# Layer norm without separate operations for mean and variance, and a third of the MLP's relus on ScalarE

## The reference

```
t = t + attn(ln(t))            # attention without softmax, 6 heads
t = t + ffn(ln(t))
ln(v)  = (v - mean(v)) / sqrt(var(v) + 1e-5)        # over the 96 numbers
ffn(x) = q16(q16(relu(q16(q8(x) @ q8(W1).T) + q8(b1))) quantised to fp8 @ q8(W2).T) + q8(b2))
```

## Time and profile before

| | |
|---|---|
| median of 3 runs | 4113.82 us (4105.76 to 4116.25) |
| profiled execution | 4110.38 us, its span 4108.6 us |
| busy PE, DVE, POOL, ACT | 3482.1, 3421.2, 2847.0, 2397.9 us (85%, 83%, 69%, 58%) |
| the block of 16 phases | from about 3393 us to the end, some 715 us |
| granted TensorE clock, whole span | 0.931 |

### The profile page before, as it was taken

One profiled execution on the slowest core, in us unless ns is written; L12 is line 12 of the kernel. 1 busy time (PEld: TensorE's weight loads), 2 busy tenths in 40 slices (PEclk: granted clock), 3 DMA queues, 4 the chain that ended last, 5 costly groups with the idle time before them and its releaser, 6 DMA issues. The chain is left out here.

```text
span 4108.6 us, 38662 instructions
## 1 busy us (share of the span) xinstructions
PE 3482.1 (85%) x10080; PEld 1402.5 (34%) x10080; DVE 3421.2 (83%) x4323; ACT 2397.9 (58%) x4121; POOL 2847.0 (69%) x2332
## 2 busy tenths in 40 slices
PE   6899999999999999999999999999860887675765
PEld 2333333333333333333333333333320334453553
DVE  3999999999999999999999999999984004778686
ACT  5666776666666677666666677666632221435445
POOL 3988889999999888999999988899870000213123
PEclk8999999999999999999999999999985999786767
DMA  2555555555556555555545555555458877100001
GB/s 85 166 157 169 163 163 159 164 168 156 160 163 176 164 162 157 156 164 157 156 154 166 162 157 163 151 158 163 145 150 207 240 236 187 47 16 12 20 1 31
DMA packets 296513, 588.62 MB, mean 143 GB/s; under 512 B 82743, under 2 KB 151994, under 8 KB 295142
## 3 DMA queue, kind: packets, MB, share of 16 engines
q1 hardware_dynamic: 229222, 516.93, 42.7%
q10 hardware_dynamic: 67072, 69.23, 6.5%
HBM read 532.16 MB, written 58.28 MB: 144 GB/s over the span
## 5 line engine op out<-in xcount | busy, mean ns | idle before, releaser
L796 POOL TENSOR_TENSOR prod<-states,c_rows 128x512 f32<-128x512 f32 x1536 | 1919.9, 1269 | 183.3 <-DVE states L726 149.2
L726 DVE TENSOR_TENSOR_SCAN states<-decay,carry,bpsum 128x512 f32<-128x512 f32 x1344 | 1676.9, 1259 | 0.0
L455 PE MATMUL ypsum<-prod,identity 128*128 128x512 f32 x3072 | 1596.4, 603 | 0.5 <-POOL prod L796 0.3
L561 ACT ACTIVATE decay<-delta,decay_rate 128x512 f32<-128x512 f32 x1344 | 934.8, 711 | 314.0 <-DVE states L726 309.4
L706 DVE TENSOR_TENSOR bpsum<-bpsum,dx 128x512 f32<-128x512 f32 x1344 | 904.6, 673 | 138.6 <-PE bpsum L448 124.4
L455 PEld LDWEIGHTS ypsum<-prod,identity 128*128 128x128 f32 x3072 | 584.2, 194 | 422.7 <-issue 280.8
L448 PE MATMUL bpsum<-b_rows,select 96*128 96x512 bf16 x1344 | 522.8, 389 | 209.4 <-DVE states L726 206.7
L448 PEld LDWEIGHTS bpsum<-b_rows,select 96*128 96x128 bf16 x1344 | 129.5, 96 | 972.6 <-DVE states L726 689.1
L1662 POOL TENSOR_TENSOR y<-y,b 128x384 f16<-128x384 f16 x64 | 68.3, 1067 | 544.8 <-ACT y L1466 544.8
L561 ACT ACTIVATE bpsum<-delta,decay_rate 128x512 f32<-128x512 f32 x192 | 132.6, 691 | 309.5 <-DVE states L726 308.6
L495 PE MATMUL mm<-h_norm,w_xs 96*128 96x512 f32 x512 | 262.8, 599 | 6.0 <-ACT h_norm L627 6.0
(11 more groups left out here) (194 smaller groups left out, 4555.9 us busy)
## 6 DMA issues: line engine op xcount, KB each, us to landing
c_rows<-bc_map SPq DMA_DIRECT2D x512, 512.0 KB, 3.8
c_rows<-bc_map SPq DMA_DIRECT2D x512, 256.0 KB, 4.0
b_wide<-bc_map ACTq DMA_DIRECT2D x128, 256.0 KB, 4.5
image<-normed_map SPq DMA_DIRECT2D x192, 96.1 KB
depthwise_map<-dw_sums ACTq DMA_DIRECT2D x96, 192.0 KB, 4.3
dw_parts<-depthwise_map SPq DMA_DIRECT2D x16, 1152.0 KB, 14.1
b_wide<-bc_map ACTq DMA_DIRECT2D x128, 128.0 KB, 4.2
normed_map<-padded SPq DMA_DIRECT2D x8, 1155.0 KB, 11.7
```

The lines of the kernel that those rows point to most:

```text
L455: pe.matmul(ypsum[:, group % Y_BANKS, :], identity[:, :], prod[:, n % P_RING, :], start=s == 0, stop=s == STATES - 1).then_inc(summed, 1)
L561: act.activation(into, delta[k % 2][:, g, :], ACT.Exp, scale=decay_rate[:, ORDER[k][0], g, s:s + 1]).then_inc(done, 1)
L726: dve.tensor_tensor_scan(states[:, n % H_RING, :], by, add, carry[:, at, u:u + 1], ALU.mult, ALU.add).then_inc(scanned, 1)
L796: pool.tensor_tensor(prod[:, n % P_RING, :], states[:, n % H_RING, :], c_rows[:, n // C_STATES % C_RING, n % C_STATES, :], ALU.mult).then_ ...
```

## The change

It has three parts. First, `center` no longer has the operation that turns the sum into a mean: one operation computes sum x (-1/96) + source. Second, `variance` ends with the sum of squares, and the root on ACT takes 1/96 as its scale and 1e-5 as its bias, read from a new one-column tile `ln_eps`. DVE sets that tile once at the start, and the three engines that waited for four start counts now wait for five. Third, bias and relu of the third piece of each chunk (k = 2) are made by ACT in place, in one operation after it has waited for its own copy, and counted by a new semaphore. DVE now makes relu 0, relu 1, and then the three casts.

```diff
-                    act.activation(stat[:, 2, tiles], stat[:, 1, tiles], ACT.Sqrt).then_inc(ln_root, 1)
+                    act.activation(stat[:, 2, tiles], stat[:, 1, tiles], ACT.Sqrt, scale=1.0 / C, bias=ln_eps[:, :]).then_inc(ln_root, 1)
...
                             act.activation(hid16[:, i % 4, :], mp[:, i % 2, :], ACT.Copy).then_inc(m_taken, 1)
+                        act.wait_ge(m_taken, i + 1)
+                        act.activation(hid16[:, i % 4, :], hid16[:, i % 4, :], ACT.Relu,
+                                       bias=b1[:, phase_of(p)[1], THIRDS - 1:THIRDS]).then_inc(last_relu, 1)
                         if c > 0:
                             add_up(c - 1)
...
                     chain(dve.tensor_reduce(stat[:, 0, tiles], src, AXIS.X, ALU.add))
-                    chain(dve.tensor_scalar(stat[:, 0, tiles], stat[:, 0, tiles], 1.0 / C, None, ALU.mult))
-                    dve.tensor_tensor(dev[:, tiles, :], src, stat[:, 0, tiles].unsqueeze(2).to_broadcast([128, SLICE, C]),
-                                      ALU.subtract).then_inc(ln_centered, 1)
+                    dve.scalar_tensor_tensor(dev[:, tiles, :], stat[:, 0, tiles].unsqueeze(2).to_broadcast([128, SLICE, C]),
+                                             -1.0 / C, src, ALU.mult, ALU.add).then_inc(ln_centered, 1)
...
-                    chain(dve.tensor_reduce(stat[:, 1, tiles], haug[:, v % 2, tiles, 0:C], AXIS.X, ALU.add))
-                    dve.tensor_scalar(stat[:, 1, tiles], stat[:, 1, tiles], 1.0 / C, LN_EPS, ALU.mult, ALU.add).then_inc(ln_var, 1)
+                    dve.tensor_reduce(stat[:, 1, tiles], haug[:, v % 2, tiles, 0:C], AXIS.X, ALU.add).then_inc(ln_var, 1)
...
-                        dve.wait_ge(hid_relu, i + 1)
+                        if k == THIRDS - 1:
+                            dve.wait_ge(last_relu, CHUNKS * n + c + 1)
+                        else:
+                            dve.wait_ge(hid_relu, 2 * (CHUNKS * n + c) + k + 1)
                         dve.tensor_copy(hid8[:, c % 2, k, :], hid16[:, i % 4, :], saturate=False).then_inc(hid8_ready, 1)
...
-                        for k in range(THIRDS):
+                        for k in range(THIRDS - 1):
...
+                        to_fp8(c, THIRDS - 2)
                         to_fp8(c, THIRDS - 1)
...
                 dve.memset(haug[:, :, :, C:C + 1], 1.0)
-                dve.wait_ge(rest_zero, 4)
+                dve.memset(ln_eps[:, :], LN_EPS).then_inc(rest_zero, 1)
+                dve.wait_ge(rest_zero, 5)
```

More of the change, by code:

```diff
@@ L1200, in batch_phase @@
         stat = sb("stat", [128, 3, TILES])
+        ln_eps = sb("ln_eps", [128, 1])
         gram = sb("gram", [128, 4, C + 1])
@@ L1205, in batch_phase @@
                  "t_full", "t_taken", "m_full", "m_taken", "dve_step", "ln_centered", "ln_squared", "ln_var", "ln_root", "ln_ready",
-                 "gram_full", "gram_step", "small_mm", "hid_relu", "hid8_ready", "y_biased", "t_step",
+                 "gram_full", "gram_step", "small_mm", "hid_relu", "last_relu", "hid8_ready", "y_biased", "t_step",
                  "out0_stored", "out1_stored", "rest_zero"]
@@ L1210, in batch_phase @@
          t_full, t_taken, m_full, m_taken, dve_step, ln_centered, ln_squared, ln_var, ln_root, ln_ready,
-         gram_full, gram_step, small_mm, hid_relu, hid8_ready, y_biased, t_step, out0_stored, out1_stored, rest_zero) = handles
+         gram_full, gram_step, small_mm, hid_relu, last_relu, hid8_ready, y_biased, t_step, out0_stored, out1_stored, rest_zero) = handles
         group_loaded = (group0_loaded, group1_loaded, group2_loaded, group3_loaded)
@@ L1395, in _ @@
                 first = 2 * CONV_GROUPS
-                pe.wait_ge(rest_zero, 4)
+                pe.wait_ge(rest_zero, 5)
                 fuse(0)
@@ L1496, in _ @@
                 first = 2 * CONV_GROUPS
-                act.wait_ge(rest_zero, 4)
+                act.wait_ge(rest_zero, 5)
                 for i in range(first):
```

## The result

| kernel | median us | lowest to highest | profiled execution | its span |
|---|---|---|---|---|
| before | 4113.82 | 4105.76 to 4116.25 | 4110.38 | 4108.6 |
| after | 4070.25 | 4065.90 to 4072.11 | 4072.11 | 4070.3 |

The medians are of five executions each. The ratio is 0.9899 with a 95% interval of 0.9888 to 0.9910, so 41.5 us less (4113.82 x 0.0101). Between the two spans the difference is 38.3 us. The medians are 43.6 us apart because the profile of before was taken in an execution 3.4 us under its median and that of after in one 1.9 us over its own.

What follows compares the result with a forecast made beforehand. DVE, partly standing still for POOL, was taken to bound seven of eight MLP phases. Seven times 3.3 us (23.1) plus 2.7 in attention, 0 in the last phase, made 26 us less: 4088 us, range 4078 to 4104.

Steps and rivals of the forecast that it cites:

- ACT's relu out of the way: MLP chunks: ACT's relu mostly fits a 0.58 us gap before y's eviction, adding 0.10 us to a chunk's loop.
- The last MLP phase: Phase without layer norm: ACT takes the lead; between 1 us less and 2 us more, 0 taken.
- Attention: Attention phases: 1.6 us less in phase 0, 0.2 in phase 1, 0.9 in six others; sum 2.7 us.
- The one behind about 0.3: Last chunk of an MLP phase, behind the five loop periods: about 0.3 us less.
- The walk: Chunk-by-chunk path through an MLP phase, pricing the third relu at 0.26 us: 2.5 us less a phase.
- the loop: MLP chunk cycle through casts, TensorE, ACT, POOL's pair and DVE: 5.34 us before, 4.98 after, 5.08 with ACT's part.
- the lower end: Gain per MLP phase from following the chunk cycle: 2.5 us; 3.3 taken, as one relu would pass before POOL's pair.
- the upper end: Gain per MLP phase from work taken off DVE: 2.1 + 0.84 + 0.76 = 3.7 us.
- The lock eats it: Rival, MLP phases: an earlier DVE only waits longer for POOL; 15 us less in all, 4099; chance 0.19.
- DVE slips past POOL: Rival, MLP chunks: two relus and a cast pass before POOL's pair; 33 us less in all, 4081; chance 0.14.
- Two passes: Rival, layer norm: fused centering makes two passes, 0.8 us more each, 26 us, all the gain; 4113; chance 0.06.
- the relu on ACT becomes the loop: Rival, MLP chunks: y, POOL and DVE queue behind ACT's relu; at 1.5 us 16 us slower, 4130; chance 0.04.

Runs made afterwards that it cites:

- e5: Changed kernel with ACT's relu of the third piece made twice, the second on its own result: 4085.69 us, ratio to before 0.9935.
- e6: Changed kernel, but ACT makes the third relu only in each MLP phase's last chunk, DVE in the others: 4085.48 us, ratio to before 0.9938.
- e10: Kernel before with only DVE's order changed to three relus, then three casts; no relu moved, layer norm as it was: 4106.77 us, ratio 0.9985.
- e3: Kernel before with POOL's two MLP additions cut to one channel of 96, so output not the reference's: 4054.94 us, ratio 0.9859.
- e4: Changed kernel with POOL's two MLP additions cut to one channel of 96, so output not the reference's: 4023.71 us, ratio to before 0.9785.
- e2: Kernel before with each chunk's third relu on ACT and casts after the relus, layer norm as it was: 4090.31 us, ratio 0.9949.
- e11: Changed kernel with a semaphore holding POOL's pair until DVE has made the next chunk's two relus: 4078.96 us, ratio to before 0.9914.
- e12: Changed kernel with a semaphore holding POOL's pair until DVE has made the next chunk's three casts: 4051.39 us, ratio to before 0.9845.

## Why the prediction was right and wrong

**Right.** What bounds the phases: DVE, with its waits for POOL counted as busy. The prices of the three new or changed operations. ACT's relu out of the way: DVE waited for it 3.3 us in 9 times in all, and the traced execution of e5 had room for nearly another. The last MLP phase: ACT leads, 0.3 us more, within the -1 to 2 given.

**Near by luck.** Attention: 3.4 us against 2.7, but not where I put it. PE's wait for the first gram of phase 0 fell from 4.44 to 1.89 us:

```profile
3471.90 0.41 PE L1341 MATMUL mp<-wv,gram 97*97 97x96 f32 x2 [1.89 <-DVE gram L1585]
```

Yet from the start of the layer norm's code to the first relu it is 133.76 us against 133.81: the 1.6 us are not there. What brought the stretches between later phases their 3.4 us stays open: in kernels with the same code there, two of them vary from 10.3 to 12.7 and from 75.8 to 80.3 us.

**Wrong: the last chunk of a phase.** "The one behind about 0.3" was mis-sized: 1.67. The walk priced the third relu by its 0.26 us of work and did not ask which operation stood there when POOL's two starts came. In that chunk the third relu and the last casts each paid 0.7 us to POOL, with nothing behind them to absorb it. 7 x (1.67 - 0.3) = 9.6 us, nearly the whole miss in the phases. e6 isolates the chunk. e10 shows which part of the change does it: with all relus left on DVE, putting the three casts behind the relus takes 1.42 us off the last chunk, and the relu's move only adds the 0.26 us that the walk had. The prediction had no term for the order of the casts; over the seven phases it is worth 7.9 us (e10), since it gives 9.9 in the last chunks and loses 2.0 elsewhere.

**Wrong in both directions: the loop.** The rest of a phase was forecast at 3.3 - 0.3 = 3.0 us. In the four phases with input to add it gave 35.51 against 39.62, less the 1.67: 2.45 us, the lower end of 2.5. There the meeting goes on as before. From the timeline of after:

```profile
3688.14 0.93 POOL L1669 TENSOR_TENSOR y<-y,b 128x384 f16<-128x384 f16 x1 [76.41 <-ACT y L1467]
3688.22 2.00 DVE L1622 TENSOR_SCALAR hid<-hid,b 128x512 f16<-128x512 f16 x2
...
3689.15 0.91 POOL L1672 TENSOR_TENSOR t<-t,y 128x384 f32<-128x384 f32 x1
...
3690.13 1.09 DVE L1616 CAST hid<-hid 128x512 fp8e5<-128x512 f16 x3
...
3691.76 0.72 ACT L1481 ACTIVATE hid<-hid,b 128x512 f16<-128x512 f16 x1
...
3692.93 0.92 POOL L1669 TENSOR_TENSOR y<-y,b 128x384 f16<-128x384 f16 x1 [2.87 <-ACT y L1467]
```

ACT's relu adds nothing to the loop: from the end of the casts (3691.22) to POOL's start it is 1.71 us, where it was 1.87. The pair of relus takes 2.00 us as at 3723.93 before, and chunks are 4.8 to 4.9 us apart (forecast 4.98 without ACT's part). I had argued for more than the lower end because one relu would pass ahead of the pair. Here none does. In the third chunk of the first two phases one does, but there a cast waits 0.71 us instead, and the chunk is no shorter (4.76 us from third cast to third cast against 4.78). In the three other phases the loop gave 5.43 - 1.67 = 3.76 us, above the 3.7 that I called the upper end:

```profile
3852.24 0.61 DVE L1622 TENSOR_SCALAR hid<-hid,b 128x512 f16<-128x512 f16 x2
...
3852.76 1.09 DVE L1616 CAST hid<-hid 128x512 fp8e5<-128x512 f16 x3
...
3853.26 1.37 POOL L1669 TENSOR_TENSOR y<-y,b 128x384 f16<-128x384 f16 x1 [81.92 <-ACT y L1467]
...
3854.75 1.68 DVE L1542 SCALAR_TENSOR_TENSOR dev_t<-stat,t 128x768 f32<-128x768 f32 x1
```

In the first chunks there is no input to add (1.4 us of DVE's time), DVE comes before POOL, and one wait (1.68 instead of 0.96 in the centering) is left where there were two. The next relus start at 3856.35, 4.1 us later. This lasts one chunk in two of the three phases and two in the other; then casts or relus pay twice as before. Against the forecast: 4 x (2.45 - 3.0) + 3 x (3.76 - 3.0) = 0.1 us, so these two misses cancel.

**The step of reasoning that failed** is "work taken from DVE: 3.7 us a phase, the upper end". Measured were 4.7 us a phase (32.8 / 7). The work taken is no bound where the engine's busy time holds 62 us of waiting: removing or shifting an operation can remove a meeting as well, each worth 0.7 us against a relu's 0.26. By e3 and e4 the change is worth 21.3 us without the lock, close to my 23.1; the 11.5 beyond it are meetings.

**The rivals.** *The lock eats it* (15 us) is refuted: in the seven phases the change is worth more with the lock than without. *DVE slips past POOL* (33 us for the whole change) named the right mechanism and gave it one microsecond in a chunk of each phase; the last chunk is that case in all seven phases, and three phases have it in their first chunks too. It put that down to when POOL starts, where e10 shows the order of the casts. It had a chance of 0.14, and it too fell short in size. *Two passes* and *the relu on ACT becomes the loop* did not occur. In e5 a second relu costs 5.4 us in the last phase and moves three of the others by 1.7 us each.

Of the rule in "ScalarE: Activation LUTs" of the Trainium skill (Rules for kernel authors) that relu belongs on VectorE, the trace bears out the direction of the prices (0.72 against 0.35 us, a factor of 2.1 for f16; the page's factor of about 3 is for bf16). Here the advice would cost time: with the third relu on ACT the seven phases are 12.8 us shorter than with the same order and the relu on DVE (e2 against e10). DVE is busy there nearly all the time, and ACT is not.

**Left open.** What decides whether POOL gets in between DVE's operations when it asks in the middle of a row of them. Three casts begun at 3558.44 run through with POOL starting at 3558.76, while three begun at 3695.32 take 2.52 us with POOL starting at 3695.55. The distance between the starts doesn't decide it: in e11 POOL starts 0.22 to 0.24 us after the first of three casts 35 times, and 25 of these rows are stopped and 10 run through. No run here separates what does. No run has the layer norm's part and the new order of casts without the relu on ACT, either. Nor was it tried to make the t sum on another engine.

## What to carry to other kernels

Where two engines lock each other out, busy time is not work: take mean minus undisturbed duration times count as the waiting, and set it beside the gain that you expect from less work. It is what the waits could cost, not what they do: before 61 of 62 us came back without the lock, after 44.6 of 54. Before pricing a removed operation by its length, look up in the timeline of each kind of iteration, the last one above all, which operation stands beside the other engine's start; a place in the order can be worth several times the work. Price a new order of the same operations as a change of its own. And then it is cheaper to move the other engine by a semaphore into a place where nobody waits (here one wait on POOL: 22.3 us in the phases) than to trim the engine that waits.

## What the hardware showed beyond what was expected

- A DVE operation that meets a POOL operation on SBUF mostly takes 0.65 to 0.72 us more, whatever its own length: relu 0.35 to 1.07, cast 0.41 to 1.14, the 8-element product 0.17 to 0.89, the centering 0.96 to 1.68. Smaller waits occur too: 0.45 us in the relus of the last phase after, 0.49 in one product of the layer norm's scaling (L1556) a phase. The reductions don't (mean 946 and 942 ns after, 946 and 943 before), and POOL beside one runs at its 0.92 us (3692.77 in e12).
- It goes the other way too: POOL's sum into t has its median at 910 ns in after and at 1506 ns in e12, where DVE's centering is under way first.
